# Three clearings on GpSimd moved off the first norm, and the second pair's shift product put behind a unit's values

## What is computed

```python
x = x + xattn(_layernorm(x), ctx_768, Wq, bq, Wk, bk, Wv, bv, Wo, bo)
x = x + attn(_layernorm(x), Wk, Wq, Wv, Wo, bo, kln_g, kln_b, qln_g, qln_b)
x = x + ffn(_layernorm(x), slot_init, w1, ...)

def xattn(query, key_value, ...):            # 16 heads of 16 channels, 4096 keys per batch
    q, k, v = (query @ Wq + bq), (key_value @ Wk + bk), (key_value @ Wv + bv)   # split in heads
    attn = softmax(clip(q k^T * 16 ** -0.5, -1e4, 1e4))
    return (attn @ v) @ Wo + bo
```

## Time and profile before

| | us |
|---|---|
| median of 3 runs | 1179.26 |
| lowest and highest of the 3 | 1169.86, 1180.69 |
| the profiled execution | 1173.13 |
| its span, first to last instruction | 1171.3 |

### The profile page before, as it was taken

One profiled execution on the slowest core, in us unless ns is written; L12 is line 12 of the kernel. 1 busy time (PEld: TensorE's weight loads), 2 busy tenths in 40 slices (PEclk: granted clock), 3 DMA queues, 4 the chain that ended last, 5 costly groups with the idle time before them and its releaser, 6 DMA issues.

```text
span 1171.3 us, 50207 instructions
## 1 busy us (share of the span) xinstructions
PE 1119.4 (96%) x22300; PEld 804.9 (69%) x22304; DVE 849.1 (72%) x1559; ACT 728.2 (62%) x1326; POOL 164.2 (14%) x200
## 2 busy tenths in 40 slices
PE   7999999999999999999999999999999997979986
PEld 5776777777777777777777777656676664646654
DVE  4777787777777777777777777778899624773553
ACT  3224776767676767676767676768878874413331
POOL 5353121111111111111111111004000003000020
PEclk9899999999999999999999999999999999999999
DMA  8666444444444444444344444322453000000001
GB/s 218 193 172 186 111 111 125 115 124 112 122 114 115 118 118 111 118 116 113 112 117 118 111 117 114 103 69 78 125 155 93 18 30 2 1 2 3 2 1 36
DMA packets 155051, 114.70 MB, mean 98 GB/s; under 512 B 17892, under 2 KB 153781, under 8 KB 154805
## 3 DMA queue, kind: packets, MB, share of 16 engines
q1 hardware_dynamic: 147795, 105.00, 33.0%
q10 hardware_dynamic: 7010, 6.23, 2.0%
HBM read 82.19 MB, written 28.84 MB: 95 GB/s over the span
## 4 chain that ended last, share of the span: by engine, by line
PE 86%; DVE 6%; ACT 4%; SPq 2%; issue 2%; DMA 1%; DVEq 0%; ACTq 0%
PE acc L1541 18%; PE st L1369 18%; PE mx L1369 16%; PE kps L1369 15%; PE st L1374 2%; PE misc L1369 2%; DVE kst L1225 2%; ACT prob L885 2%; PE mx L1374 1%; PE kps L1374 1%; PE setB L1782 1%; PE acc L1374 1%; PE st L1696 1%; PE setB L1791 1%; ACT prob L794 1%
## 5 line engine op out<-in xcount | busy, mean ns | idle before, releaser
L977 DVE TENSOR_REDUCE mxp<-mx 128x1 f32<-128x512 f32 x959 | 626.0, 686 | 177.5 <-PE mx L1369 154.5
L1369 PE MATMUL st<-qst,kst 99*32 99x256 bf16 x8192 | 423.9, 272 | 1.2 <-ACT prob L794 1.1
L794 ACT ACTIVATE prob<-st 128x512 f32<-128x512 f32 x544 | 305.9, 598 | 113.4 <-PE st L1369 110.1
L1369 PE MATMUL mx<-kst,qst 96*32 96x512 bf16 x3532 | 371.0, 380 | 1.9 <-DMA kst<-kscr 0.7
L1369 PEld LDWEIGHTS st<-qst,kst 99*32 99x32 bf16 x8192 | 271.7, 97 | 116.1 <-ACT prob L794 4.4
L794 ACT ACTIVATE xn<-st 128x512 f32<-128x512 f32 x240 | 135.8, 597 | 75.3 <-PE st L1369 75.1
L794 ACT ACTIVATE xnT<-st 128x512 f32<-128x512 f32 x240 | 141.4, 598 | 38.1 <-PE st L1369 35.2
L1541 PE MATMUL acc<-prob,v_raw 128*17 128x256 f32 x2176 | 144.6, 378 | 2.8 <-ACT prob L794 2.8
L1369 PEld LDWEIGHTS mx<-kst,qst 96*32 96x32 bf16 x3532 | 119.0, 94 | 7.0 <-DVE mxp L977 4.9
L534 POOL CAST kraw<-kraw 128x512 bf16<-128x512 f32 x50 | 30.7, 614 | 562.8 <-DVE kraw L939 562.8
L1369 PE MATMUL kps<-wv,ctx 128*32 128x256 f32 (+1 forms) x1504 | 100.9, 380 | 0.0
(11 more groups left out here) (386 smaller groups left out, 1073.0 us busy)
## 6 DMA issues: line engine op xcount, KB each, us to landing
kst<-kscr SPq DMA_DIRECT2D x120, 192.0 KB, 2.9
kst<-kscr SPq DMA_DIRECT2D x360, 64.0 KB, 2.8
kscr<-kraw SPq DMA_DIRECT2D x100, 192.0 KB, 2.7
ctx<-in_ctxT SPq DMA_DIRECT2D x93, 128.0 KB, 2.6
ctx<-in_ctxT SPq DMA_DIRECT2D x93, 64.0 KB, 3.0
kscr<-prob SPq DMA_DIRECT2D x16, 192.0 KB, 3.5
kscr<-o_sb SPq DMA_DIRECT2D x12, 192.0 KB, 3.3
qscr<-v_raw SPq DMA_DIRECT2D x8, 192.0 KB, 2.5
```

What stands on the lines that cost most here:

```text
L794: act.activation(exps(n), st[n % 3][:, :], ACT.Exp).then_inc(exp_done, 1)
L977: dve.reduce_max(at, bank_of_max(n)[:, :], AX.X).then_inc(max_red, 1)
L1369: mm = pe.matmul(to[32 * c:32 * c + 32, :], weights[:, 32 * c:32 * c + 32], moving, start=start, stop=stop, skip_group_check=True)
```

## The change

Three edits.

The clearing of `low_vh` moves from behind the last group into GpSimd's pass for group 14, behind that group's release. It waits there until all values of group 14 are through, which TensorE does at t = 2 of group 15. The part of `kst` that it clears holds blocks of keys that no unit of group 15 reads.

The clearings of `v2e` and `v2o` now wait for the end of the last group, for the turned `o_sb`, and also for all eight scaled tiles of the first norm. They stand together, and `add_bias(1)` behind them as before.

The second pair's `turn_shift` moves on TensorE from t = 61 to t = 62 of each group but the last (15 times), where it follows the values product of that iteration.

```diff
@@ -637,10 +637,15 @@
+                if q == NQ - 2:
+
+                    pool.wait_ge(pv_done, 16 * (NQ - 1))
+                    pool.memset(low_vh[:, 0:2048], 0.0).then_inc(sel_set, 1)
+
             pool.wait_ge(pv_done, 16 * NQ)
-            pool.memset(low_vh[:, 0:2048], 0.0).then_inc(sel_set, 1)
+            pool.wait_ge(xnT_ps, 8)
+            pool.wait_ge(ln_xn, 2 * NT)
             pool.memset(v2e, 0.0).then_inc(v2_zero, 1)
-            pool.wait_ge(xnT_ps, 8)
             pool.memset(v2o, 0.0).then_inc(v2_zero, 1)
             add_bias(1)
             add_bias(2)
@@ -1667,7 +1672,7 @@
                 if t == 59 and q + 1 < NQ:
                     turn_shift(q + 1, 0)
-                if t == 61 and q + 1 < NQ:
+                if t == 62 and q + 1 < NQ:
                     turn_shift(q + 1, 1)
```

## The result

The changed kernel takes 1169.36 us (median of 20 executions, 1162.85 to 1174.46), the kernel before 1174.53 us (20 executions, 1168.30 to 1181.94). The ratio is 0.9946 with a 95% interval of 0.9928 to 0.9964, so 4.2 to 8.5 us less, 6.3 in the middle. That is under 1%. The forecast was 1171.7 us with a gain of 4.5 us.

What follows compares the result with a forecast made beforehand. TensorE, busy 96% of the span, was taken as the bound; 2.4 us (norm) plus 2.2 (three ends) less 0.1 (release) made 4.5, from 1176.2 to 1171.7 us, range 1163 to 1179.

Steps and rivals of the forecast that it cites:

- The norm: Behind the last group: with two clearings moved away, VectorE's first scaled pair takes 0.73 instead of 3.17 us, gaining 2.4 us.
- the third gives nothing: First norm: moving the third clearing gains nothing, since the next copy waits 0.23 us for TensorE anyway.
- all three slow pairs: First norm: all three slow VectorE pairs lie beside a GpSimd clearing, none free of one is slow; clearings taken as cause.
- moves by about 2.4 us: First norm: the chain behind the faster scaled pair moves by about 2.4 us, perhaps 2.3.
- The ends of groups 11 to 13: Ends without projections: TensorE work of 1.31 us covers its 0.83 us stand; 0.75 us an end, 3 x 0.75 = 2.2 us.
- flag, release and values come up to 0.83 us sooner too: Group 12's start: the last maximum unit comes 0.83 us sooner, so what follows its flag does too, up to 0.83 us.
- The release of group 15: Group 15's start: GpSimd's flag load overlaps the moved clearing; cost 0 to 1.4 us, taken as 0.1 us.
- ScalarE took nothing at the ends: Rival: ScalarE takes the gain at the ends, TensorE waiting at t = 2 to 8; gain 2.3 us, 1173.9, chance 0.22.
- The release did not wait for the clearing: Rival: group 15's release waits for the clearing, 1.4 us lost; gain 3.2 us, 1173.0, chance 0.15.
- The later product held nobody: Rival: the later shift product holds ScalarE in every group, 19.7 us lost, less 2.4; 1193.5, chance 0.03.
- The clearings were the cause: Rival: the clearings weren't what slowed VectorE at the norm, only the ends gain, 2.1 us; 1174.1, chance 0.03.
- wrong if the span falls by less than 2 us or more than 6: Sign for the whole execution: the prediction is wrong if the span falls by less than 2 us or more than 6.

Runs made afterwards that it cites:

- e3_busy: Kernel before with 12 matmuls that nobody reads put into TensorE's wait for `o_sb` behind the last group; 1175.61 us, ratio 0.9990.
- e8: Changed kernel without GpSimd's reading of the flag, `low_vh`'s clearing one group later, second shift product back at unit 61; 1169.48 us, ratio 0.9940.
- e4: Changed kernel without GpSimd's reading of the flag (value load, branch, clipping code), and with `low_vh`'s clearing one group later; 1166.44 us, ratio 0.9903.
- e1: Kernel before with only the three clearings moved, the shift product staying at t = 61; 1173.78 us, ratio 0.9981.
- e0: The changed kernel, unaltered, timed and profiled a second time; 1170.89 us, ratio 0.9951 against the kernel before.
- e2: Kernel before with only the second pair's shift product moved to t = 62, the clearings staying; 1173.26 us, ratio 0.9979.
- e6: Changed kernel with `low_vh`'s clearing one group later, behind the release of group 15 and no longer ahead of it; 1169.71 us, ratio 0.9949.
- e10_wo_later: Changed kernel with SyncE's last weight load (256 KB) issued two eighths of a group later, after unit 15 of group 14; 1168.94 us, ratio 0.9954.

## Why the prediction was right

**The norm: right, and one term short.** The pair from 3.17 to 0.73 us, the wait down by 2.43 us, the forecast 2.4. The clearings end 5.0 us ahead of `values_out` (4.8 forecast), the third gives nothing, and VectorE's copy beside them isn't held. One reading of the rows was wrong without harm: "all three slow pairs" are two pairs, 3.17 and 1.68 us, with three slow instructions in them (1.28, 1.97 and 1.37 us). Each of the three lies beside a clearing, so the argument stands. What was missing is the clock: 1.41 us, shown by e3_busy. The step that failed is the sentence that the chain "moves by about 2.4 us": it took the work behind the wait to be as long as before.

**The ends of groups 11 to 13: right in mechanism, mis-sized.** The cover works as it said: 0.83 to 0.86 us an end when nothing else gates (e8 against e4). The term was 3 x 0.75 = 2.2 us. Taking the profiles of before, e1 and e3 (13.53, 13.71 and 13.29 us in the last) against those of after, e0, e2 and e6 (12.78, 12.54 and 13.49 in the last), ends 11 and 12 gave 0.7 and 0.9 us, and end 13 lost 0.15, 1.5 us in all. The failing step is "flag, release and values come up to 0.83 us sooner too". It took the release to stay 3.0 us behind the flag. At groups 12 and 13 it stayed about there (3.0 to 3.5 in these four); at group 14 it became 4.0 to 4.2 us, for a weight load in front of the code fetch (e10_wo_later). Ends 10 and 14 gave about 0.2 us each, where the prediction counted 0.

**The release of group 15: right.** The clearing starts at 930.95 with the values product's semaphore (forecast about 932 before the gain of 1.1 us up to there), the load overlaps it, and the release is 2.9 us behind. It cost nothing; the forecast had 0.1 us.

**The rivals.** ScalarE took nothing at the ends: without the release they fall by the full 0.85 us. The release did not wait for the clearing. The later product held nobody. The clearings were the cause, as one clearing and none show. All four fell.

**The numbers.** The terms as the runs size them: 2.4 for the norm, 1.4 for the clock, 1.5 for the three ends and 0.4 for the ends beside them make 5.7 us, within 4.2 to 8.5. So the forecast gain of 4.5 us comes near by two errors that partly cancel: 1.8 us missing (the clock and ends 10 and 14) and 0.7 us too much (end 13). The range of 1163 to 1179 us was so wide that no gain at all would have lain in it; the mechanism is borne out by the stretches, not by the time. The forecast of 1171.7 us stood 2.3 us above the result: 1.7 us because the middle of four executions, 1176.2, was above the median of twenty, 1174.5, which is chance, and 0.7 us because the gain (5.2 us between the medians) was more than 4.5. One of its own tests was badly made: "wrong if the span falls by less than 2 us or more than 6" would have called it wrong by the one profiled pair (1.3 us), although the norm and ends 11 and 12 moved as it said. For the same reason its 1168.6 us for the profiled execution, taken from 1173.13, missed: the profiled execution of the changed kernel took 1171.81. The kernel before spreads over 13.6 us from one execution to the next, mostly by the clock.

## What to carry to other kernels

Where an engine's instruction is far slower than its twin next to it, look for a GpSimd instruction that ends just before it does, and move that. Then compare the rows behind the wait with the same rows elsewhere, since a wait can cost a second time by TensorE's clock. When a gain at the start of a group should come through a branch on GpSimd, ask what SyncE issues in the microsecond behind the branch, or take the branch off the path altogether.

## What the hardware showed beyond what I expected

- A branch on GpSimd behind a loaded value costs 2.9 to 4.2 us here from the load to the release, of which the load is 0.3 (median); the release follows the landing of an instruction packet by 0.8 to 1.7 us in 172 of 176 cases. At group 8, where two packets come one behind the other, it is 5.0 to 6.0 us. A 256 KB load issued 0.1 us behind the flag delays it by 0.9 us (4.1 against 3.3, e10_wo_later).
- A GpSimd clearing that has begun holds VectorE's scaling until 0.15 us behind its own end, in all four cases looked at; a free one takes 0.40 us, one held 1.28 to 1.97 us.
- GpSimd's load of a value and the fetch behind it run beside its own clearing (both start at 930.9; the clearing lasts 1.80 us, the release comes at 933.8).
- After TensorE had worked 0.33 of 3.7 us its clock was granted at half for 3.4 us, in e2_shift for 6.8 us. After a wait of 1.82 us it wasn't.
- The mean granted clock of an execution lies between 0.984 and 1.000, so 0 to 37 of 1170 us run at half clock, at places that change from one profiled execution to the next. This makes most of the spread of the times: the executions of one kernel scatter by 2.6 to 4.0 us (standard deviation), and by 0.9 to 1.7 us with the clock taken out.
